# Loads of 112 rows in a convolution kernel with group norm: partitions 8 to 119, with a zero scale on the others

## The chip, the cores and the metric

The kernel runs on one core of a Trainium2 chip. The core has TensorE (PE), VectorE (DVE), ScalarE (ACT), GpSimd (POOL) and SyncE (SP), which here issues all DMAs; 16 DMA engines move data between the memory of the chip (HBM) and the on-chip memory of 128 partitions. The metric is the device time of one execution in microseconds. The kernel before takes 844.32 us, the median of 3 runs (842.21 to 863.63).

## What is computed

The input x has 32 images of 384 channels, 56 x 56 each, in float32. It is normalised in 32 groups of 12 channels, convolved channel by channel with a filter as tall as the image that wraps around, given a bias, and added to x.

```python
def _gn(v, G=32, eps=1e-5):
    g = v.reshape(B_, G, C_ // G, H_, W_)
    m = jnp.mean(g, axis=(2, 3, 4), keepdims=True)
    s = jnp.var(g, axis=(2, 3, 4), keepdims=True)
    return ((g - m) / jnp.sqrt(s + eps)).reshape(v.shape)

x_cat = jnp.concatenate([x, x[:, :, :-1, :]], axis=2)          # the wrap in H
out = conv_general_dilated(x_cat, weight, (1, 1), 'VALID', feature_group_count=C)
x + (out + bias[None, :, None, None])                          # conv of _gn(x)
```

## The kernel before

**Tiling.** The image rows (H = 56) lie on partitions. Two image sets lie side by side: one on partitions 8 to 63, the other on 64 to 119 (EDGE = 8, SIDE = 64, DATA = 112 rows). Partitions 0 to 7 and 120 to 127 hold no data; the host pads x with zeros there, so a load brings 128 rows. A unit is one group of 12 channels for 16 images (8 on each side); there are 64 units, two for a group. A unit is loaded and stored in two halves of 6 channels, 2688 floats to a partition each.

**The matmul.** The convolution in H is a product with a 128 x 128 matrix for each channel, two circulant blocks, one for each side. The matrices of a group lie in `runs` (two buffers). The taps come by DMA onto partitions 64 to 127 for output columns 64 to 119, and DVE's `lay_out` copies them to partitions 0 to 63 for the columns of the other side. The rows of this matrix on partitions 120 to 127 are not zero, nor are those on 0 to 7, so `xn`, the normalised input, has to be zero there.

**The stages of a unit**, each on its engine, in the order in which the engine's program is written:

- SP loads into one of six slots of `xt` (XS = 6). It waits until the store that emptied the slot has landed. One in-order queue holds stores, loads and the taps: for each half of unit u the store of (u, h) and then the load of (u + 5, h).
- DVE takes statistics (`bn_stats`, L280) three units ahead, 16 instructions a unit, and adds conv, bias and x for the even channels into `xt` (L304).
- POOL and PE combine the statistics over partitions with the matrices `neg_mean`, `avg` and `avg_dev`, whose columns for the outer partitions are zero, so that mean and variance are zero there. POOL's `newton` turns variance into `rstd` and `shift`: ACT takes the root of var + eps, DVE the reciprocal r0, and POOL does one Newton step with 1.5 from `three_halves`.
- ACT normalises `xt` into `xn` one unit ahead (L355), and moves the odd channels from PSUM to `kept` (L364), which POOL adds to `xt` (L248).
- PE multiplies the 12 channels into six banks of PSUM.

On the outer partitions DVE and POOL write bias and conv into the loaded tile too; the next 128-row load overwrites it with zeros. The store takes the 112 data rows alone.

**The start.** DVE sets eps (L272) and zeroes `runs`; POOL builds the three matrices and `three_halves` (L195 to L208) in a chain. ACT, PE and POOL wait for both through `consts_set`.

Of the kernel before, what the change touches and what calls it, by code (L numbers as in the profile page):

```python
# [13 lines left out]
GROUPS = 32  # L14
CG = C // GROUPS
EPS = 1e-5

# [3 lines left out]
P = 128  # L23
SIDE = P // PAR
EDGE = SIDE - H
DATA = PAR * H
# [11 lines left out]
BLOCK = SIDE * CG  # L38
RUN = H * CG
TAPS = PAR * BLOCK  # L40

XS = 6
# [12 lines left out]
def through(channels, u, c):  # L55

    return u * len(channels) + sum(k <= c for k in channels)

def build(nc, x, taps, bias, out):  # L60
    with ExitStack() as ctx:
        def sb(name, shape):
            return ctx.enter_context(nc.sbuf_tensor(name, shape, F32))
# [4 lines left out]
        def sem(name):  # L68
            return ctx.enter_context(nc.semaphore(name))

        xt = sb("xt", [P, XS, HALVES, FREE])
        xn = sb("xn", [P, NS, HALVES, FREE])
        kept = sb("kept", [P, KEEP, N])
        runs = sb("runs", [P, 2, TAPS])
# [4 lines left out]
        eps = sb("eps", [P, 1])  # L79
        warm = sb("warm", [P, 1])  # L80
        three_halves = sb("three_halves", [P, BP])
# [17 lines left out]
        x_loaded = [[sem(f"x_loaded{s}_{h}") for h in range(HALVES)] for s in range(XS)]  # L99
# [3 lines left out]
        consts_set = sem("consts_set")  # L103
# [38 lines left out]
        @block.sync  # L142
        def _(sp):
            def load(n, h):
                if n >= UNITS:
                    return
                if n >= XS:
                    sp.wait_ge(out_stored[n % XS][h], 16 * (n // XS))
                sp.dma_start(xt[:, n % XS, h, :], x[n, :, h, :]).then_inc(x_loaded[n % XS][h], 16)

            def load_taps(g):

                sp.dma_start(runs[SIDE:P, g % 2, BLOCK:BLOCK + RUN], taps[g]).then_inc(taps_loaded[g % 2], 16)

            def store(u, h):
                last = (h + 1) * CH - 1
                sp.wait_ge(dve_taken, through(DVE_CH, u, last))
                sp.wait_ge(pool_added, through(ACT_CH, u, last))
                sp.dma_start(out[u, :, h, :], xt[EDGE:EDGE + DATA, u % XS, h, :]).then_inc(out_stored[u % XS][h], 16)

            for h in range(HALVES):
                load(0, h)
            for h in range(HALVES):
                load(1, h)
            sp.wait_ge(runs_zeroed, 1)
            load_taps(0)
            sp.dma_start(bias_all[:], bias.broadcast_to([P, C])).then_inc(bias_loaded, 16)
            for n in range(2, XS):
                for h in range(HALVES):
                    load(n, h)  # L170
                if n == 3:
                    load_taps(1)

            for u in range(UNITS):
                for h in range(HALVES):
                    store(u, h)
                    g = u // PER_GROUP + 2
                    if h == 1 and u % PER_GROUP == PER_GROUP - 1 and g < GROUPS:
                        load_taps(g)

                    if u >= 1:
                        load(u - 1 + XS, h)
            for s in range(XS):
                for h in range(HALVES):
                    sp.wait_ge(out_stored[s][h], 16 * len(range(s, UNITS, XS)))

        @block.gpsimd
        def _(pool):
            link = itertools.count(1)

            def chained(ins):
                ins.then_inc(pool_link, 1)
                pool.wait_ge(pool_link, next(link))
# [4 lines left out]
            for m in (neg_mean, avg, avg_dev):  # L198
# [3 lines left out]
                for first in (EDGE, SIDE):  # L202
# [2 lines left out]
                                                    base=-first, pattern=[[0, H]], channel_multiplier=1))  # L205
                    chained(nc.gpsimd.affine_select(out=cols, in_=cols, compare_op=ALU.is_ge, fill=0.0,
                                                    base=first + H - 1, pattern=[[0, H]], channel_multiplier=-1))
            nc.gpsimd.memset(three_halves[:], 1.5).then_inc(consts_set, 1)  # L208
            pool.wait_ge(consts_set, 2)

            def add_means(n):
                r = n % RS
# [20 lines left out]
            def newton(n):  # L233
                r = n % RS
                pool.wait_ge(var_ready, n + 1)
                chained(nc.gpsimd.tensor_scalar(hv[:], var[:, r, :], EPS, -0.5, ALU.add, ALU.mult))  # L236
                pool.wait_ge(r0_ready, n + 1)
# [18 lines left out]
            for u in range(UNITS):  # L256
                n = u + LEAD_COEF
# [11 lines left out]

        @block.vector  # L270
        def _(dve):
            nc.vector.memset(eps[:], EPS).then_inc(consts_set, 1)  # L272
            nc.vector.memset(runs[:], 0.0).then_inc(runs_zeroed, 1)

            def stats(n, k0, k1):
# [8 lines left out]
            def lay_out(g):  # L284

                dve.wait_ge(taps_loaded[g % 2], 16 * (g // 2 + 1))
                side = runs[SIDE:P, g % 2, BLOCK:BLOCK + RUN]
                nc.vector.tensor_copy(runs[0:SIDE, g % 2, 0:RUN], side)  # L288
                nc.vector.tensor_copy(runs[0:SIDE, g % 2, RUN:BLOCK], side[:, 0:BLOCK - RUN]).then_inc(taps_laid, 1)  # L289

            def add_vars(n):
# [20 lines left out]
            invert(0)  # L312
            stats(1, ALL * 3 // 4, ALL)
            lay_out(0)
            stats(2, 0, ALL // 2)
            add_vars(1)
# [20 lines left out]
        def _(act):  # L337
# [26 lines left out]
                nc.scalar.activation(kept_of(u, c), bank_bw(c), ACT.Identity, bias=bias_of(u, c)  # L364
                                     ).then_inc(act_evicted, 1)

            act.wait_ge(consts_set, 2)
            nc.scalar.activation(warm[:], eps[:], ACT.Sqrt)
            negmean(0)
            root(0)  # L370
# [6 lines left out]
            for u in range(UNITS):  # L377
                n, m = u + LEAD_NORM, u + LEAD_COEF
# [22 lines left out]
        def _(pe):  # L401
# [26 lines left out]
                nc.tensor.matmul(bank(c), lay[:, :, c], channel_of(xn, u % NS, c), start=True, stop=True  # L428
                                 ).then_inc(conv_ready, 1)

            pe.wait_ge(consts_set, 2)
            for n in range(LEAD_COEF):
                mean(n)
                variance(n)
# [1 line left out]
            for u in range(UNITS):  # L436
                n = u + LEAD_COEF
# [39 lines left out]
```

## Time and profile before

| | |
|---|---|
| median of 3 runs | 844.32 us |
| the profiled execution | 843.1 us, of which its span 841.4 us |
| busy: PE, DVE, ACT, POOL | 706.6, 727.6, 661.6, 574.5 us |
| bytes moved | 336.57 MB, of which HBM read 181.86, written 154.14 |
| mean rate over the span | 400 GB/s |
| TensorE's granted clock, mean | 0.995 |

The busy time of an engine is its share of one profiled execution. The DMA share is the mean busy share of the 16 DMA engines; with that share near 1 the GB/s beside it is what they can do on that mix, and a rate divided by the share compares stretches in which the engines were not full. A waiting row names what was waited for, the total, the count and the longest. A row for a stretch lists its start and end, its length, then busy time and instructions of PE, PE's weight loads, DVE, ACT and POOL, and last the granted clock, the DMA share and GB/s.

### The profile page before, as it was taken

Reading aid. Unit: us, or ns where it says so; the run is one execution under the profiler, and the core shown is the slowest. Engines: PE = TensorE matmul, PEld = TensorE weight load, DVE = VectorE, ACT = ScalarE, POOL = GpSimd, SP = SyncE. Lnnn points to the kernel's source line nnn. Section 1 sums busy time; section 2 is a strip of 40 time slices with the busy share of each in tenths; the row PEclk is TensorE's granted clock in tenths of the full one; section 3 lists DMA queues with packets and bytes.
Section 4 is the critical chain, followed back from the end, with each engine's and each line's share of the span. In section 5 each row is a group of like instructions: output and inputs, shape, how many; then the busy total and the mean of one; then the engine's idle time right before and its main releaser. Section 6 shows DMA issues by size and latency. Waiting matters only on the chain.

```text
span 841.4 us, 8606 instructions
## 1 busy us (share of the span) xinstructions
PE 706.6 (84%) x1920; PEld 555.5 (66%) x1920; DVE 727.6 (86%) x1602; ACT 661.6 (79%) x1026; POOL 574.5 (68%) x1114
## 2 busy tenths in 40 slices
PE   0699889888887888988888988888988888987895
PEld 0477667666666666766666767666766667766684
DVE  7799988888888888889998899998888998898862
ACT  0799878777787777878878988887887887887893
POOL 3388667767676666766766776776776676775775
PEclk9999999999999999999999999999999999999998
DMA  8999999999999999999999999999999999999977
GB/s 349 411 350 400 411 411 414 416 422 409 412 413 396 402 402 390 398 403 410 414 418 415 417 413 419 425 418 420 418 414 419 422 418 414 410 420 404 391 243 248
DMA packets 37572, 336.57 MB, mean 400 GB/s; under 512 B 4624, under 2 KB 4752, under 8 KB 6800
## 3 DMA queue, kind: packets, MB, share of 16 engines
q1 hardware_dynamic: 37520, 336.02, 98.9%
q8 instruction: 15, 0.25, 0.1%
q14 instruction: 37, 0.30, 0.1%
HBM read 181.86 MB, written 154.14 MB: 399 GB/s over the span
## 4 chain that ended last, share of the span: by engine, by line
DMA 57%; DVE 19%; ACT 11%; issue 6%; POOL 5%; PE 1%; SPq 0%; POOLq 0%
DMA xt<-x 31%; DMA out<-xt 26%; DVE st L280 10%; ACT xn L355 7%; DVE xt L304 5%; ACT kept L364 3%; POOL xt L248 3%; DVE runs L289 2%; PE conv L428 1%; DVE runs L288 1%; POOL newt L240 0%; POOL newt L239 0%; POOL rstd L241 0%; POOL shift L242 0%; POOL newt L238 0%
## 5 line engine op out<-in xcount | busy, mean ns | idle before, releaser
L428 PE MATMUL conv<-xn,runs 128*128 128x448 f32 x1536 | 662.3, 574 | 64.7 <-ACT xn L355 48.7
L428 PEld LDWEIGHTS conv<-xn,runs 128*128 128x128 f32 x1536 | 511.3, 347 | 147.4 <-ACT xn L355 77.0
L280 DVE BATCH_NORM_STATS2 st<-xt 128x6 f32<-128x336 f32 x1024 | 451.9, 495 | 84.8 <-DMA xt<-x 83.3
L248 POOL TENSOR_TENSOR xt<-xt,kept 128x448 f32<-128x448 f32 x384 | 434.7, 1139 | 104.5 <-ACT kept L364 104.5
L355 ACT ACTIVATE xn<-xt,shift,rstd 128x672 f32<-128x672 f32 x512 | 462.7, 942 | 47.2 <-POOL shift L242 47.2
L304 DVE SCALAR_TENSOR_TENSOR xt<-conv,bias_all,xt 128x448 f32<-128x448 f32 x384 | 257.0, 669 | 17.9 <-PE conv L428 17.8
L364 ACT ACTIVATE kept<-conv,bias_all 128x448 f32<-128x448 f32 x384 | 232.8, 620 | 9.6 <-PE conv L428 9.4
L345 ACT ACTIVATE std<-var,eps 128x8 f32<-128x8 f32 x64 | 19.2, 301 | 97.3 <-DVE var L294 97.2
L404 PEld LDWEIGHTS p_mean<-msum,neg_mean 128*128 128x128 f32 x128 | 19.9, 193 | 94.5 <-POOL msum L217 80.2
L404 PE MATMUL p_mean<-msum,neg_mean 128*128 128x8 f32 x128 | 25.2, 269 | 59.2 <-POOL msum L217 59.2
L238 POOL TENSOR_TENSOR newt<-r 128x8 f32<-128x8 f32 x64 | 12.7, 198 | 62.1 <-DVE r L299 61.4
L236 POOL TENSOR_SCALAR hv<-var 128x8 f32<-128x8 f32 x64 | 12.6, 196 | 52.5 <-DVE var L294 49.9
L412 PEld LDWEIGHTS p_var<-st,avg 128*128 128x128 f32 x128 | 19.6, 192 | 35.4 <-POOL dev L231 35.0
L289 DVE COPY runs<-runs 64x96 f32<-64x96 f32 x32 | 29.2, 912 | 0.0
L288 DVE COPY runs<-runs 64x672 f32<-64x672 f32 x32 | 27.9, 872 | 1.2
L412 PE MATMUL p_var<-st,avg 128*128 128x32 f32 x128 | 26.6, 291 | 2.8 <-POOL dev L231 2.8
L227 POOL TENSOR_TENSOR dev<-st,nmean 128x16 f32<-128x16 f32 x128 | 25.6, 221 | 1.9 <-ACT nmean L340 1.9
L413 PE MATMUL p_var<-dev,avg_dev 128*128 128x32 f32 x128 | 25.3, 280 | 0.0
L214 POOL TENSOR_TENSOR mpart<-st 128x16 f32<-128x16 f32 x64 | 15.2, 237 | 7.6 <-DVE st L280 7.6
L340 ACT COPY nmean<-p_mean 128x8 f32<-128x8 f32 x64 | 9.5, 149 | 13.4 <-PE p_mean L404 13.2
L413 PEld LDWEIGHTS p_var<-dev,avg_dev 128*128 128x128 f32 x128 | 19.9, 196 | 0.0
L231 POOL TENSOR_TENSOR dev<-dev 128x32 f32<-128x32 f32 x64 | 15.2, 238 | 5.0
(31 smaller groups left out, 97.2 us busy)
## 6 DMA issues: line engine op xcount, KB each, us to landing
xt<-x SPq DMA_DIRECT2D x128, 1344.0 KB, 16.0
out<-xt SPq DMA_DIRECT2D x128, 1176.0 KB, 14.3
runs<-taps SPq DMA_DIRECT2D x32, 168.0 KB, 13.5
bias_all<-bias SPq DMA_DIRECT2D x1, 192.0 KB, 13.8
```

The lines of the kernel that those rows point to most:

```text
L227: ins = nc.gpsimd.tensor_tensor(d[:, h], means, nm, ALU.add)
L248: nc.gpsimd.tensor_tensor(cell, cell, kept_of(u, c), ALU.add).then_inc(pool_added, 1)
L280: ins = nc.vector.bn_stats(st[:, n % RS, h, b, :], xt[0:P, n % XS, h, b * ROW:(b + 1) * ROW])
L288: nc.vector.tensor_copy(runs[0:SIDE, g % 2, 0:RUN], side)
L289: nc.vector.tensor_copy(runs[0:SIDE, g % 2, RUN:BLOCK], side[:, 0:BLOCK - RUN]).then_inc(taps_laid, 1)
L304: nc.vector.scalar_tensor_tensor(out=cell, in0=bank_bw(c), scalar=bias_of(u, c), in1=cell, op0=ALU.add, op1=ALU.add).then_inc(dve_taken, 1)
L355: ins = nc.scalar.activation(xn[:, n % NS, :, part], xt[0:P, n % XS, :, part], ACT.Identity, scale=rstd[:, n % RS, b:b + 1], bias=shift[:, ...
L364: nc.scalar.activation(kept_of(u, c), bank_bw(c), ACT.Identity, bias=bias_of(u, c)).then_inc(act_evicted, 1)
L404: nc.tensor.matmul(p_mean[:, n % RS * BP:(n % RS + 1) * BP], neg_mean[:], msum[:, n % RS, :], start=True, stop=True).then_inc(mean_ready, 1)
L412: nc.tensor.matmul(dst, avg[:], squares, start=True, stop=False)
L413: nc.tensor.matmul(dst, avg_dev[:], dev[:, r, :], start=False, stop=True).then_inc(pvar_ready, 1)
L428: nc.tensor.matmul(bank(c), lay[:, :, c], channel_of(xn, u % NS, c), start=True, stop=True).then_inc(conv_ready, 1)
```

## The change

A load into a slot that has held data before covers rows 8 to 119 alone, on the same partitions as the stores. The first load into each slot still covers all 128 rows. The outer partitions are thus not cleared after that; bias and conv pile up on them. So that `xn` stays zero there, `eps` is 1e32 and `three_halves` is 0 on the outer partitions: r0 becomes 1e-16, the Newton step multiplies it by nearly nothing, and `rstd` is zero. `lay_out` leaves the columns of output partitions 0 to 7 as the zeros that `runs` was set to, so its first copy has 576 columns in place of 672.

```diff
@@ -146,7 +150,8 @@
                     return
                 if n >= XS:
                     sp.wait_ge(out_stored[n % XS][h], 16 * (n // XS))
-                sp.dma_start(xt[:, n % XS, h, :], x[n, :, h, :]).then_inc(x_loaded[n % XS][h], 16)
+                rows = slice(0, P) if n < XS else slice(EDGE, EDGE + DATA)
+                sp.dma_start(xt[rows, n % XS, h, :], x[n, rows, h, :]).then_inc(x_loaded[n % XS][h], 16)
 
             def load_taps(g):
 
@@ -205,8 +210,15 @@
                                                     base=-first, pattern=[[0, H]], channel_multiplier=1))
                     chained(nc.gpsimd.affine_select(out=cols, in_=cols, compare_op=ALU.is_ge, fill=0.0,
                                                     base=first + H - 1, pattern=[[0, H]], channel_multiplier=-1))
-            nc.gpsimd.memset(three_halves[:], 1.5).then_inc(consts_set, 1)
-            pool.wait_ge(consts_set, 2)
+            chained(nc.gpsimd.memset(eps[:], EPS))
+            chained(nc.gpsimd.memset(eps[P - 32:P], FAR))
+            chained(nc.gpsimd.memset(eps[P - 32:EDGE + DATA], EPS))
+            chained(nc.gpsimd.memset(eps[0:EDGE], FAR))
+            chained(nc.gpsimd.memset(three_halves[:], 1.5))
+            chained(nc.gpsimd.memset(three_halves[P - 32:P], 0.0))
+            chained(nc.gpsimd.memset(three_halves[P - 32:EDGE + DATA], 1.5))
+            nc.gpsimd.memset(three_halves[0:EDGE], 0.0).then_inc(consts_set, 1)
+            pool.wait_ge(consts_set, 1)
 
             def add_means(n):
                 r = n % RS
@@ -269,7 +281,6 @@
 
         @block.vector
         def _(dve):
-            nc.vector.memset(eps[:], EPS).then_inc(consts_set, 1)
             nc.vector.memset(runs[:], 0.0).then_inc(runs_zeroed, 1)
 
             def stats(n, k0, k1):
@@ -285,7 +296,7 @@
 
                 dve.wait_ge(taps_loaded[g % 2], 16 * (g // 2 + 1))
                 side = runs[SIDE:P, g % 2, BLOCK:BLOCK + RUN]
-                nc.vector.tensor_copy(runs[0:SIDE, g % 2, 0:RUN], side)
+                nc.vector.tensor_copy(runs[0:SIDE, g % 2, BLOCK - RUN:RUN], side[:, BLOCK - RUN:RUN])
                 nc.vector.tensor_copy(runs[0:SIDE, g % 2, RUN:BLOCK], side[:, 0:BLOCK - RUN]).then_inc(taps_laid, 1)
 
             def add_vars(n):
@@ -364,7 +375,7 @@
                 nc.scalar.activation(kept_of(u, c), bank_bw(c), ACT.Identity, bias=bias_of(u, c)
                                      ).then_inc(act_evicted, 1)
 
-            act.wait_ge(consts_set, 2)
+            act.wait_ge(consts_set, 1)
             nc.scalar.activation(warm[:], eps[:], ACT.Sqrt)
             negmean(0)
             root(0)
@@ -428,7 +439,7 @@
                 nc.tensor.matmul(bank(c), lay[:, :, c], channel_of(xn, u % NS, c), start=True, stop=True
                                  ).then_inc(conv_ready, 1)
 
-            pe.wait_ge(consts_set, 2)
+            pe.wait_ge(consts_set, 1)
             for n in range(LEAD_COEF):
                 mean(n)
                 variance(n)
```

(`FAR = 1e32` is new beside the other constants.)

On SP's queue, from the first store on (its source is `xt`, its target `out`; loads go from `x` to `xt`), the kernel before issues:

```order
L159 DMA out<-xt 112x2688 [waits pool_added,dve_taken] x3
L149 DMA xt<-x 128x2688 [waits out_stored0_0]
L159 DMA out<-xt 112x2688 [waits pool_added,dve_taken]
L153 DMA runs<-taps 64x672
L149 DMA xt<-x 128x2688 [waits out_stored0_1]
```

After the change the same place reads:

```order
L164 DMA out<-xt 112x2688 [waits pool_added,dve_taken] x3
L154 DMA xt<-x 112x2688 [waits out_stored0_0]
L164 DMA out<-xt 112x2688 [waits pool_added,dve_taken]
L158 DMA runs<-taps 64x672
L154 DMA xt<-x 112x2688 [waits out_stored0_1]
```

No DMA has moved and every wait is the same; each load that waits for a store has 112 rows where it had 128. The twelve loads ahead of this place are unchanged.

On POOL, at the end of the constants and before the first statistics are combined (`mpart`), the kernel before has:

```order
L206 AFFINE_SELECT avg_dev<-avg_dev 128x56 [waits pool_link]
L204 AFFINE_SELECT avg_dev<-avg_dev 128x56 [waits pool_link]
L206 AFFINE_SELECT avg_dev<-avg_dev 128x56 [waits pool_link]
L208 MEMSET three_halves 128x8 [waits pool_link]
L214 TENSOR_TENSOR mpart<-st 128x16 [waits stats_ready,consts_set]
```

And after the change:

```order
L211 AFFINE_SELECT avg_dev<-avg_dev 128x56 [waits pool_link]
L213 MEMSET eps 128x1 [waits pool_link]
L214 MEMSET eps 32x1 [waits pool_link]
L215 MEMSET eps 24x1 [waits pool_link]
L216 MEMSET eps 8x1 [waits pool_link]
L217 MEMSET three_halves 128x8 [waits pool_link]
L218 MEMSET three_halves 32x8 [waits pool_link]
L219 MEMSET three_halves 24x8 [waits pool_link]
L220 MEMSET three_halves 8x8 [waits pool_link]
L226 TENSOR_TENSOR mpart<-st 128x16 [waits stats_ready,consts_set]
```

Seven memsets are added to the chain at this one place; POOL's program behind it is unchanged.

## Rows read from the trace of the kernel before

**Rows 1.** The page: busy time by engine, packets and queue.

```profile
PE 706.6 (84%) x1920; PEld 555.5 (66%) x1920; DVE 727.6 (86%) x1602; ACT 661.6 (79%) x1026; POOL 574.5 (68%) x1114
...
DMA packets 37572, 336.57 MB, mean 400 GB/s; under 512 B 4624, under 2 KB 4752, under 8 KB 6800
...
q1 hardware_dynamic: 37520, 336.02, 98.9%
...
HBM read 181.86 MB, written 154.14 MB: 399 GB/s over the span
```

**Rows 2.** The page: the chain that ended last, shares by engine.

```profile
DMA 57%; DVE 19%; ACT 11%; issue 6%; POOL 5%; PE 1%; SPq 0%; POOLq 0%
```

**Rows 3.** DVE's waits (us, times, longest) and busy time, 100 to 780 us.

```profile
DVE st L280 <- DMA xt<-x: 76.3, 72, 2.4
...
100.00:780.00 680.00, 589.17 (x1596) 459.37 (x1596) 600.31 (x1330) 548.15 (x852) 473.40 (x909) 1.00 1.01 412
```

**Rows 4.** DMA to landing: loads from 40 us on, then the last five stores.

```profile
L149 SPq DMA_DIRECT2D xt<-x x116: 351/361/2477, 51.4 to 782.9; - x116
...
DMA to landing us min/median/max: 10.3/15.9/18.5
...
L159 SPq DMA_DIRECT2D out<-xt x5: 316/317/317, 817.2 to 835.3; - x5
...
DMA to landing us min/median/max: 5.3/5.3/5.5
```

**Rows 5.** The chain, one loop (start us, length us, what).

```profile
571.06 15.16 DMA out<-xt
586.24 15.94 DMA xt<-x
602.20 1.33 DVE st L280 x3
...
621.33 15.25 DMA out<-xt
```

**Rows 6.** The page: DMA issues, KB each; then all loads' landing, min/median/max.

```profile
xt<-x SPq DMA_DIRECT2D x128, 1344.0 KB, 16.0
out<-xt SPq DMA_DIRECT2D x128, 1176.0 KB, 14.3
runs<-taps SPq DMA_DIRECT2D x32, 168.0 KB, 13.5
...
DMA to landing us min/median/max: 5.8/16.0/32.4
```

**Rows 7.** Busy by stretch, clock, DMA share, GB/s: loads alone, refill, stores alone.

```profile
8.00:12.00 4.00, 0.00 (x0) 0.00 (x0) 4.00 (x11) 0.00 (x0) 0.00 (x0) 1.00 1.01 430
44.00:68.00 24.00, 22.31 (x66) 18.20 (x64) 23.91 (x55) 22.50 (x35) 19.85 (x38) 1.00 0.97 339
800.00:841.00 41.00, 31.55 (x85) 26.70 (x83) 19.04 (x33) 26.85 (x42) 27.18 (x38) 0.94 0.73 247
```

**Rows 8.** The same view: two mixed stretches.

```profile
200.00:400.00 200.00, 169.19 (x456) 131.29 (x456) 171.69 (x385) 156.54 (x244) 134.04 (x259) 1.00 1.01 404
400.00:600.00 200.00, 176.03 (x482) 138.66 (x482) 182.72 (x402) 164.89 (x257) 142.37 (x274) 1.00 1.01 418
```

**Rows 9.** DVE by line: busy us, mean ns.

```profile
L288 DVE COPY runs<-runs 64x672 f32<-64x672 f32 x32 | 27.9, 872 | 1.2
```

**Rows 10.** The first 15 us in order of time (start us, length us).

```profile
1.58 0.10 POOL L200 MEMSET neg_mean<- 128x8 f32 x1
1.75 0.10 POOL L201 MEMSET neg_mean<- 128x8 f32 x1
...
6.17 0.10 POOL L208 MEMSET three_halves<- 128x8 f32 x1
6.30 0.20 ACT L368 ACTIVATE warm<-eps 128x1 f32<-128x1 f32 x1 [4.23 <-POOL three_halves L208]
...
13.42 0.23 POOL L214 TENSOR_TENSOR mpart<-st 128x16 f32<-128x16 f32 x1 [7.15 <-DVE st L280]
...
14.68 0.17 ACT L340 COPY nmean<-p_mean 128x8 f32<-128x8 f32 x1 [8.18 <-PE p_mean L404]
```

More of the change, by code:

```diff
@@ L16 @@
 EPS = 1e-5
+FAR = 1e32
 PAR = 2
```

## The prediction

> **What bounds the kernel now.** I read the page first. The DMA queue that carries all loads and stores keeps the 16 engines busy for 98.9% of the span, while the busiest compute engine, DVE, works 86% of it [rows 1]. The chain that ended last agrees: 57% of it is DMA and only 19% is DVE [rows 2]. So this is a kernel whose transfers set the pace, unless the DMA share is queueing behind something else. Three further views say that it is not.
>
> The waits of DVE between 100 and 780 us have a single entry, the x load, with 76.3 us; DVE is busy 600.3 of those 680 us, so all but 680 - 600.3 - 76.3 = 3.4 us of its idle time is that wait [rows 3]. The DMA share of that stretch is 1.01 (full) at 412 GB/s [rows 3]. And a DMA takes 15.9 us from issue to landing for a load in the middle of the kernel, 15.2 and 16.0 us in a piece of the chain, but only 5.3 us for a store when nothing else is under way at the end [rows 4, 5]. Ten of those 16 us are thus time in the queue. The chain repeats one loop every four units: store issued at 571.06, landed, its slot's load landed at 602.20, then DVE, POOL, ACT and POOL again until the next store at 621.33 [rows 5]. That is 50.3 us, of which 31.1 is DMA and 19.1 compute. Without a queue the loop would be about 19 + 5.3 + 5.8 = 30 us (5.8 is the shortest landing of a load [rows 6]), or 7.6 us a unit. So neither the number of slots nor latency is the limit: the bytes are.
>
> One unit carries two loads of 1344 KB, two stores of 1176 KB and half a taps load of 168 KB [rows 6], 5124 KB = 5.247 MB. At 412 GB/s that is 12.73 us. DVE needs 600.3 us of work in the same 680, and 680 / 12.73 = 53.4 units, so 11.24 us a unit. These two numbers, 12.73 and 11.24, are the case: the DMA can lose up to 1.5 us a unit before DVE sets the pace.
>
> **The change part by part.** *The loads.* Twelve loads (six slots, two halves) keep 128 rows. The other 128 - 12 = 116 lose 16 rows of 128, which is 168 KB or 0.172 MB each: 116 x 0.172 = 19.96 MB of the 336.57 MB [rows 1, 6]. The order on SP's queue and its waits stay as they were. If the rate stays 412 GB/s, the saving is 19.96 MB / 412 GB/s = 48.4 us. The unit falls to 5.247 - 0.344 = 4.903 MB, 11.90 us. DVE's 11.24 still fits under it, with 0.66 us to spare where 1.5 us was.
>
> *The rate.* This is where it could fail. Loads of 128 rows, before any store is issued (8 to 12 us), run at 430 GB/s with share 1.01, so 426 per full share. Stores alone, which are 112 rows from partition 8 (from 800 us on), run at 247 GB/s with share 0.73: 338 per full share, a fifth less [rows 7]. Part of the 0.73 is that they come singly, but the rate per busy share should not fall for that. So something about a 112-row transfer costs time when it runs by itself, and the trace can't say whether it is the direction (a store) or the shape. The loads now get that shape. There is one hint against fear: in the steady stretches, where stores are nearly half the bytes, the whole mix makes 418 GB/s at 1.01 (414 per full share) from 400 to 600 us, and 404 from 200 to 400 [rows 8]. If loads take their 426 there, the stores must take 2.408 MB / (5.247 / 414 - 2.839 / 426) = 2.408 / 6.009 us = 401 GB/s, not 338. The penalty of the shape is mostly gone once the queue is deep. In contrast, from 44 to 68 us, when stores begin and the queue is refilled, the mix makes only 339 at 0.97 [rows 7].
>
> The cost of the shape is therefore bounded from both sides. Nothing: 48.4 us are saved. All of it, as in the tail: a load of 1.204 MB at 338 takes 3.56 us against 1.376 / 426 = 3.23, so each of the 116 is 0.33 us longer and the kernel 38 us slower. At the stores' steady 401 GB/s it is 3.00 us, and the saving is 116 x 0.23 = 27 us; but that charges to stores everything that slows the mix, some of which (the refill, memory, loads themselves) falls on loads already. I take the value nearest to the steady rows, a loss of 5 us out of the 48.4. It is the deep queue that decides, and the change leaves it deep: 11.90 against DVE's 11.24.
>
> The Trainium skill, "SBUF — State Buffer", section "Door 1: The DMA port swizzle", speaks against this change. It says that partitions share 16 ports of eight partitions each, that a transfer is as fast as the ports it reaches, and its table puts partitions 0 to 7 and 120 to 127 on four ports that each serve four other partitions in 8 to 119; by its arithmetic twelve ports still carry eight rows and nothing is saved. The tail's 338 GB/s agrees with it in direction; the steady 414 doesn't show it, because loads and stores alternate there and no port is asked for all the time. By that rule alone the sum would be about the time of before (R2 below).
>
> *The taps copy.* Each of the 32 layouts copies 576 columns in place of 672: 872 ns x 96 / 672 = 0.12 us, 4 us of DVE in all, 0.06 us a unit [rows 9]. DVE waits for DMA, so this is nothing on the path; it widens DVE's spare time to 0.7 us.
>
> *The constants.* POOL sets eps and three_halves with eight chained memsets where one stood, and DVE loses one. A small memset on POOL takes 0.10 us and starts 0.17 us after the one before it, so consts_set comes 7 x 0.17 = 1.2 us later, at about 7.5 us. Behind it wait POOL's first mpart, which waits for statistics until 13.42 anyway, and ACT's warm-up at 6.30, whose next work is at 14.68 [rows 10]. Hidden with 6 us of cover; 1.2 us if that were gone. The zero in rstd on the outer partitions adds no instruction.
>
> *DVE's waits that return.* With 0.7 us of spare a unit instead of 1.5, a burst in which DMA is quick no longer helps: DVE can't catch up. From 200 to 400 us DMA ran at 404 and from 400 to 600 at 418 [rows 8], so the spare varies by 5.247 x (1/404 - 1/418) = 0.43 us a unit, less than 0.7. I allow 2 us.
>
> The sum against the profiled span: 841.4 - 48.4 + 5 + 2 = 800.0 us of span. The profiled execution itself took 1.7 us more than its span (843.1), and the median of the runs is 844.3, so 1.7 to 2.9 us are added: about 802. I say 801.
>
> **The rivals.** *R1, DVE becomes the bound.* If the loads came for nothing, the span would be at least 841.4 - 76.3 - 4 = 761 us. That is below 800, so DVE alone can't stop the gain. But the two paces are only 6% apart, and when DVE holds the stores back the queue drains, transfers run singly and their rate falls towards that of 44 to 68 us. For: that stretch exists, with DVE busy 23.9 of 24 us [rows 7]. Against: it ended by itself at 68 us. Half of the gain would be gone: 841.4 - 24 = 817, a time of 819. The DMA share would be 0.95 to 0.98 and DVE's wait for x small.
>
> *R2, the shape is paid for in full by the ports.* A 112-row load takes as long as a 128-row one did (373 GB/s in place of 426). The bytes fall and the time doesn't: 841 to 844 us. For: the tail's 338. Against: the mixed stretches. The rate on the page would fall from 400 to 316.6 MB / 841 us = 376 GB/s at a full share.
>
> *R3, slower.* Loads of 112 rows collide with each other as stores do when they are alone, at more than 3.23 us each; that is the point from which it decides. At the tail's 338 GB/s the price is 38 us: 879 to 882. For it speaks that now no transfer in the queue has the regular 128-row shape. Against it: the queue is mostly full and half of it is the other direction, as it is for stores now.
>
> **How the numbers follow.** A measurement of this kernel can tell about 2% from no change, so faster is below 827.4 and slower above 861.2. Forecast (bytes decide, 790 to 810): 0.60. R1 (810 to 827): 0.18. R2 (827 to 861): 0.12. R3 (over 861): 0.10. The first two are faster: 0.78. The low end of the range: a steady rate of 425 GB/s, the loads' 426, in place of 412 would take off a further 20 us, but with DVE at 11.2 of then 11.5 us a unit some 4 of it would come back; 784. The high end takes in R1 and the first part of R2, up to the saving being a third: 832. That leaves out some 0.19.
>
> **What would show it.** The page should list 316.6 MB, reads about 162 MB, DMA share in the steady stretch still 1.00 or more, and 405 to 418 GB/s there. DVE's wait for x should fall from 76 to about 35 to 45 us in the steady part, and the loop of the chain from 50.3 to 47 us. A load's landing should shorten from 15.9 to about 14.5 us. The startup should be the same to 1 us. R1 shows a share below 1 and DVE near 95%; R2 and R3 show a full share at under 385 GB/s with DVE's wait for x as long as now or longer. The prediction is wrong if the mean time of a byte in the queue changes with the shape of the load.

## The result and the profile after

The changed kernel takes 889.4 us (median, 886.8 to 905.6), the kernel before beside it 848.5 us. The ratio is 1.050, with a 95% interval of 1.038 to 1.062: slower by 5%, where a gain of 5% was forecast. Executions of one kernel scatter (842 to 864 us before), so ratios here compare the faster executions of each. The profiled execution's span is 889.2 us.

The page after, lines that answer to [rows 1, 2, 6]; the second is GB/s in 40 slices of the span:

```profile
PE 726.2 (82%) x1920; PEld 562.1 (63%) x1920; DVE 716.6 (81%) x1601; ACT 663.0 (75%) x1026; POOL 575.8 (65%) x1121
...
GB/s 353 412 315 356 353 365 382 371 360 367 341 367 385 381 361 377 403 391 339 347 351 333 324 343 345 352 354 366 346 356 341 340 379 364 360 371 392 396 253 252
DMA packets 35716, 316.61 MB, mean 356 GB/s; under 512 B 4624, under 2 KB 4752, under 8 KB 6800
...
q1 hardware_dynamic: 35664, 316.07, 98.8%
...
DMA 71%; DVE 10%; POOL 7%; ACT 6%; issue 3%; PE 1%; SPq 0%; POOLq 0%
...
xt<-x SPq DMA_DIRECT2D x116, 1176.0 KB, 17.5
```

The bytes are as forecast, 316.61 MB. The 16 engines are as full as before, 98.8%, but they move 356 GB/s where they moved 400. The rate wanders between 324 and 403 after the start. DMA's share of the chain has gone from 57 to 71%. A load takes 17.5 us to land, not the 14.5 that were forecast.

DVE's wait from 100 to 780 us, then stretches of the same execution (columns as in [rows 3, 7]):

```profile
DVE st L291 <- DMA xt<-x: 126.7, 92, 3.3
...
8.00:12.00 4.00, 0.00 (x0) 0.00 (x0) 4.00 (x11) 0.00 (x0) 0.00 (x0) 1.00 1.01 427
100.00:780.00 680.00, 565.93 (x1481) 432.69 (x1482) 550.51 (x1239) 511.25 (x793) 440.07 (x844) 0.95 1.01 359
400.00:600.00 200.00, 164.09 (x421) 123.71 (x420) 153.98 (x350) 144.13 (x224) 123.58 (x238) 0.93 1.01 343
850.00:889.00 39.00, 29.31 (x78) 24.95 (x78) 16.75 (x28) 24.92 (x38) 25.82 (x36) 0.96 0.71 239
```

Against [rows 3]: DVE's wait for x is 126.7 us, not 76.3, and the steady rate 359, not 412. The first row, full loads alone, is nearly unchanged (427, 430 before), and so is the tail of stores alone (239 at a share of 0.71, which is 337 per full share; 338 before). The loss lies in the stretch where 112-row loads and stores share the queue: 4.903 MB at 359 GB/s is 13.7 us a unit, against 12.7 before.

The kept traces also have one record for each packet, and nearly all packets are rows of 10,752 bytes. From 100 to 780 us such a packet takes 404 ns at the median in both kernels. But 27% of them take over 500 ns after the change, where 5% did before, and their mean is 481 ns, not 419. That ratio, 1.148, is the ratio of the two rates (412 / 359). So the engines do not stand idle between packets; some packets of the same size take longer.

### The profile page after: what moved, and what is told of

The parts are those of the page before. It is cut to its first block, busy times and chain, and to the rows that moved or that the text cites. A ratio compares the mean times of both kernels' runs of the same rounds, so it can differ in the third digit from the quotient of the medians.

```text
span 889.2 us, 8612 instructions
## 1 busy us (share of the span) xinstructions
PE 726.2 (82%) x1920; PEld 562.1 (63%) x1920; DVE 716.6 (81%) x1601; ACT 663.0 (75%) x1026; POOL 575.8 (65%) x1121
## 2 busy tenths in 40 slices
DMA packets 35716, 316.61 MB, mean 356 GB/s; under 512 B 4624, under 2 KB 4752, under 8 KB 6800
## 3 DMA queue, kind: packets, MB, share of 16 engines
q1 hardware_dynamic: 35664, 316.07, 98.8%
## 4 chain that ended last, share of the span: by engine, by line
DMA 71%; DVE 10%; POOL 7%; ACT 6%; issue 3%; PE 1%; SPq 0%; POOLq 0%
DMA xt<-x 40%; DMA out<-xt 32%; DVE st L291 6%; ACT xn L366 4%; POOL xt L260 4%; DVE xt L315 3%; ACT kept L375 2%; PE conv L439 1%; DVE runs L299 0%; POOL newt L252 0%; POOL newt L251 0%; POOL rstd L253 0%; POOL newt L250 0%; POOL shift L254 0%; DVE runs L284 0%
## 5 line engine op out<-in xcount | busy, mean ns | idle before, releaser
L439 PE MATMUL conv<-xn,runs 128*128 128x448 f32 x1536 | 688.1, 592 | 104.0 <-ACT xn L366 92.7
L315 DVE SCALAR_TENSOR_TENSOR xt<-conv,bias_all,xt 128x448 f32<-128x448 f32 x384 | 256.5, 668 | 18.9 <-PE conv L439 18.8
L415 PEld LDWEIGHTS p_mean<-msum,neg_mean 128*128 128x128 f32 x128 | 23.5, 216 | 86.6 <-POOL msum L229 67.2
L415 PE MATMUL p_mean<-msum,neg_mean 128*128 128x8 f32 x128 | 25.2, 270 | 48.4 <-POOL msum L229 48.4
L250 POOL TENSOR_TENSOR newt<-r 128x8 f32<-128x8 f32 x64 | 12.7, 199 | 75.9 <-DVE r L310 75.4
L299 DVE COPY runs<-runs 64x576 f32<-64x576 f32 x32 | 29.8, 932 | 2.0 <-DMA runs<-taps 1.1
L252 POOL TENSOR_TENSOR newt<-newt,three_halves 128x8 f32<-128x8 f32 x64 | 13.0, 204 | 5.0
(37 smaller groups left out, 98.8 us busy)
## 6 DMA issues: line engine op xcount, KB each, us to landing
out<-xt SPq DMA_DIRECT2D x128, 1176.0 KB, 15.7
xt<-x SPq DMA_DIRECT2D x116, 1176.0 KB, 17.5
```

Of the source, the lines that this page charges most:

```text
L299: nc.vector.tensor_copy(runs[0:SIDE, g % 2, BLOCK - RUN:RUN], side[:, BLOCK - RUN:RUN])
L315: nc.vector.scalar_tensor_tensor(out=cell, in0=bank_bw(c), scalar=bias_of(u, c), in1=cell, op0=ALU.add, op1=ALU.add).then_inc(dve_taken, 1)
L415: nc.tensor.matmul(p_mean[:, n % RS * BP:(n % RS + 1) * BP], neg_mean[:], msum[:, n % RS, :], start=True, stop=True).then_inc(mean_ready, 1)
```

## The experiments

**Which edit.** The first run undoes the loads alone.

```diff
-rows = slice(0, P) if n < XS else slice(EDGE, EDGE + DATA)
+rows = slice(0, P)
```

> The changed kernel with every load at 128 rows again; eps, three_halves, the constants in POOL and the shorter taps copy stay as changed. If the loads alone are the cause (S, D or Q): the time of the kernel before, 840 to 848 us, steady rate about 412 GB/s. If the startup or the other edits cost something: over 855.

848.6 us, ratio 1.005 (0.999 to 1.011). The other edits cost nothing that can be measured; all of the loss comes from the loads. (The profiled execution took 873.9 us, so the steady rate of 412 that was expected can't be read from it.)

**What a DMA of each shape can do.** This kernel has no compute. It reads and writes the same arrays by the same queue, in most phases with five DMAs under way. Each kernel of DMAs alone in this document was executed once. The phases:

```python
PHASES = [  # kind, load rows, at, store rows, at, under way, count
    ("L", P, 0, None, 0, 5, 16), ("L", DATA, EDGE, None, 0, 5, 16),
    ("S", None, 0, P, 0, 5, 16), ("S", None, 0, DATA, EDGE, 5, 16),
    ("M", P, 0, DATA, EDGE, 5, 32), ("M", DATA, EDGE, DATA, EDGE, 5, 32), ...
```

> DMA alone, no compute; the output is not the reference's. After 12 loads of 128 rows come 12 phases, each drained before the next: loads of 128 rows; loads of 112 rows (partitions 8 to 119); stores of 128; stores of 112; then alternating stores and loads: 128-row loads with 112-row stores (as before), 112 with 112 (as after), 128 with 128, 112-row loads with 128-row stores; loads of 64 rows from the same source onto partitions 0 to 63, then onto 32 to 95; and the 112/112 mix again with 3 and with 8 DMAs under way instead of 5. Theory S (the shape costs: transfers of 112 rows collide in the on-chip memory, whichever their direction): per full share, 128-row loads and stores 420 to 426 GB/s, 112-row loads and stores both 340 to 380, the mixes with one regular side 400 to 420, 128/128 420 to 426, 112/112 340 to 375; 64 rows at 32 about twice as fast as at 0. Theory D (stores are slow as such): stores 340 at either height, 112-row loads 426, 112/112 no slower per byte than 128/112. Theory Q (depth of the queue decides): the 112/112 mix is slow at 3 and reaches 400 or more at 8.

One row inside each phase, in the order of the text above; the 128/128 mix (417) is left out (columns: stretch, length, POOL, clock, DMA share, GB/s):

```profile
46.00:94.00 48.00, 0.00 (x0) 1.00 1.01 427
100.00:162.00 62.00, 0.00 (x0) 1.00 1.01 292
169.00:216.00 47.00, 0.00 (x0) 1.00 1.01 422
223.00:278.00 55.00, 0.00 (x0) 1.00 0.97 330
290.00:380.00 90.00, 0.00 (x0) 1.00 1.01 419
395.00:495.00 100.00, 0.00 (x0) 1.00 1.00 362
615.00:720.00 105.00, 0.00 (x0) 1.00 1.01 370
730.00:778.00 48.00, 0.00 (x0) 1.00 1.02 207
785.00:808.00 23.00, 0.00 (x0) 1.00 1.01 428
815.00:915.00 100.00, 0.00 (x0) 1.00 1.01 368
925.00:1022.00 97.00, 0.00 (x0) 1.00 1.01 375
```

Loads: 427 GB/s at 128 rows, 292 at 112. Stores: 422 and 330. So the shape costs and the direction doesn't: Theory D falls with the third row. A 112-row load is hit even harder than a store, 292 against 330, where 340 to 380 was expected for both. The mix of before makes 419, that of after 362, and its mirror image (112-row loads, 128-row stores) 370 with the same bytes as before. The last two are averages over a rise that I did not see at first: in slices of about 20 us the mix of after goes from 341 to 376 and the mirror image from 343 to 390.

The two rows of 207 and 428 are the cleanest pair: the same 64 source rows to partitions 0 to 63 make 207, to 32 to 95 they make 428. Only the place in the on-chip memory differs. In the packet records a row takes 839 ns at the median in the first of the two and 404 in the second; in the 112-row loads it takes 574, in the 128-row loads 405.

The Trainium skill, "SBUF — State Buffer", section "Door 1: The DMA port swizzle", gives the table behind that pair: 0 to 63 reach eight of 16 ports, 32 to 95 all of them. The trace agrees, 207 against 428.

Depth does not remove the loss: 368 with three under way, 375 with eight, though both rise too (344 to 383, and 343 to 410).

**Stores at 128 rows in the kernel.** From the kernel before, with an output array of 128 rows:

```diff
-sp.dma_start(out[u, :, h, :], xt[EDGE:EDGE + DATA, u % XS, h, :])
+sp.dma_start(out[u, :, h, :], xt[:, u % XS, h, :])
```

> The kernel before with stores of 128 rows too (the output array has 128 rows, the host drops 16). Bytes 358.6 MB, 6.5% more. Theory S: the rate in the steady part rises from 412 to 422 to 426, the tail (stores alone) from 338 to about 420 per full share; a unit takes 5.59 MB / 424 = 13.2 us in place of 12.73, the kernel about 868 us. Theory D: tail still 338 per share, steady rate at most 412, 890 us or more.

```profile
100.00:780.00 680.00, 572.31 (x1530) 441.37 (x1530) 576.88 (x1275) 525.93 (x818) 454.70 (x868) 0.99 1.01 421
832.00:872.00 40.00, 30.29 (x81) 25.34 (x79) 18.69 (x33) 26.23 (x40) 26.48 (x38) 0.96 0.70 291
```

873.5 us, ratio 1.030 (1.024 to 1.035), for 6.5% more bytes. The steady rate is 421, and the tail of stores alone makes 291 at a share of 0.70, 416 per full share, against 338 in [rows 7]. The tail that I had read as possibly the direction was the shape.

**Half the loads, and the mirror image.** Only the first half of each unit at 112 rows:

```diff
-rows = slice(0, P) if n < XS else slice(EDGE, EDGE + DATA)
+rows = slice(0, P) if n < XS or h == 1 else slice(EDGE, EDGE + DATA)
```

> The changed kernel, but only the loads of the first half of a unit have 112 rows, those of the second 128. Bytes 326.6 MB. If every 112-row load costs its own extra time (as measured, 45 us for 116 of them, against 48 us that fewer bytes should have saved): half of it, ratio about 1.025, 866 us. If the collisions need loads and stores that all have the irregular shape, and one regular DMA in four sets them straight: nothing lost and 24 us saved, about 820.

Ratio 1.073 (1.057 to 1.089), 919.8 us: worse than all of them at 112. The page says why: 357 GB/s on average, the rate of the changed kernel (356), with 10 MB more to move. So the price is not one per 112-row load. I read it as a state of the whole queue that half the loads are enough to bring about; what brings it about is not shown. Both expectations missed: the 866 us from a price for each load, and the 820 us from the idea that one regular DMA in four would set the rest straight.

The mirror image has the stores of 128 rows above on top of the changed kernel.

> The changed kernel with stores of 128 rows: one direction regular, the other not, the mirror image of the kernel before, and within 1% its bytes (loads 2 x 1176 KB and stores 2 x 1344 KB a unit). Theory that one irregular direction is harmless: ratio 1.00 to 1.02. By the DMA-only phases (370 GB/s for this mix against 419 for the mix of before): 5.247 MB / 370 = 14.2 us a unit in place of 12.7, so about 930 us, ratio 1.10.

Four executions took 891, 896, 926 and 936 us, the kernel before beside them 839 to 868. The profiled one (891) runs at 358 GB/s from 100 to 330 us and at 404 from 350 to 840. Two of the four are near the 930 us expected from the DMA-only 370, two are not. One irregular direction is thus not harmless when it is the loads; and the state can change within one execution.

**Where the rows lie.** More phases, six shapes of loads first:

```python
PHASES = [  # pattern of (kind, rows, at, source row), under way, count
    ([("L", 112, 8, 8)], 5, 16), ([("L", 112, 8, 0)], 5, 16), ([("L", 112, 0, 8)], 5, 16),
    ([("L", 96, 16, 8)], 5, 16), ([("L", 64, 8, 8)], 5, 16), ([("L", 48, 32, 8)], 5, 16), ...
```

> DMA alone again, 12 phases after the 12 full loads; its output is not the reference's. Six kinds of loads alone, 16 each: 112 rows to partitions 8 to 119; the same but from source rows 0 to 111; the same to partitions 0 to 111; 96 rows to 16 to 111; 64 rows to 8 to 71; 48 rows to 32 to 79. Then 12 times a load of 64 rows to 32 to 95 with one of 24 rows to 8 and one of 24 to 96. Then mixes: 112-row stores with 128-row loads; with 112-row loads; store, 112-row load, store, 128-row load; 112-row stores with 64-row loads to 32; and with 64-row loads to 8. For the pattern with 112- and 128-row loads in turn, a model with whole packets waiting for each other gives 353, below the 362 of all 112 and the 419 of all 128. Rival H (the source side): source rows 0 to 111 at 420. Rival E (only the rows that start at 8 are bad): 112 rows to 0 and 96 to 16 at 420.

```profile
46.00:110.00 64.00, 0.00 (x0) 1.00 1.01 280
118.00:175.00 57.00, 0.00 (x0) 1.00 1.01 304
184.00:245.00 61.00, 0.00 (x0) 1.00 1.01 290
254.00:310.00 56.00, 0.00 (x0) 1.00 1.01 258
320.00:368.00 48.00, 0.00 (x0) 1.00 1.01 203
575.00:672.00 97.00, 0.00 (x0) 1.00 1.00 379
682.00:780.00 98.00, 0.00 (x0) 1.00 1.01 388
790.00:860.00 70.00, 0.00 (x0) 1.00 1.00 383
876.00:960.00 84.00, 0.00 (x0) 1.00 0.99 345
```

The first five rows are loads alone, the sixth and seventh the mixes with 112-row loads and with both kinds, the last two those with 64-row loads to 32 and to 8. (The 48-row phase ran at 251, the three-piece loads at 254, the mix with 128-row loads at 420.) No start and no source helps 112 or 96 rows: 280, 304, 290, 258. Rivals H and E fall. What no phase separates is the side on which 112 rows collide: each still goes between HBM and the on-chip memory, and H changed only the first source row. That it is the on-chip side, as with 64 rows, is argued.

The port-bound 64 rows at 8 make 203, as forecast. The mix that alternates 112- and 128-row loads makes 388 here, between the two pure mixes (379 and 420). In the kernel with half of the loads at 112 rows the same order made only 357, and that difference is open. My model of whole packets that wait for each other had put it below both, at 353; it misses. The 112/112 mix, 362 before, averages 379 here and has come to 416 in its last 22 us.

**The same in the kernel**, with 64-row loads (48 data rows of each repeated load are left out):

```diff
-rows = slice(0, P) if n < XS else slice(EDGE, EDGE + DATA)
+rows = slice(0, P) if n < XS else slice(8, 72)      # and slice(32, 96)
```

> The changed kernel, but repeated loads bring only 64 rows to partitions 32 to 95, so 48 data rows are left out of each load; all engines work as before. 3.87 MB a unit. Port theory: loads are regular, DMA at about 400 needs 9.7 us a unit, DVE's 11.3 sets the pace: 765 to 790 us.

> The same number of rows and bytes, but to partitions 8 to 71. Port theory: a 64-row load takes 0.688 MB / 207 = 3.3 us in place of 1.6, as long as a 128-row load, so about 12.7 us a unit or more: 840 to 900 us. If only bytes and rows count: the same as with partitions 32 to 95.

747.6 us to 32 and 748.1 to 8: no difference, and both expectations (765 to 790, and 840 to 900) missed. I had used the rate of such loads alone for a kernel in which they alternate with stores; the DMA-only mixes had made 383 and 345. The rows from 100 to 650 us, to 32 and to 8:

```profile
100.00:650.00 550.00, 522.91 (x1495) 434.52 (x1494) 547.35 (x1244) 513.15 (x798) 447.78 (x844) 1.00 0.99 351
100.00:650.00 550.00, 522.21 (x1492) 433.90 (x1491) 546.82 (x1243) 512.61 (x796) 448.70 (x844) 1.00 1.01 351
```

DVE works 547 of 550 us in both. (The chain that ended last runs through ACT for 52% and hardly through DVE; that DVE is the bound is read from its busy time.) The time of this pair could not tell the places apart, but the landing does: a load takes 9.3 us to 32 and 12.0 us to 8. The pair measured two other things. With DVE as the bound the span is 745 us. And to 32 the DMA share is 0.99 at 351 GB/s, where the same mix alone makes 383: a share near 1 says that something is always under way, and not that the engines can do no more. So the GB/s beside such a share is not always what they can do on that mix, as I wrote ahead of the prediction.

**Can the bad state end?** The next kernel keeps 112/112 up for 96 DMAs and tries groups and two queues.

> DMA alone, the output is not the reference's; stores always 112 rows. After the 12 full loads: 112-row loads from SP's queue beside stores from ACT's queue (16 each, 3 and 2 under way); 128-row loads beside such stores in the same way; then on SP's queue alone: store and load in turn at 112/112, 96 of them (to see whether the rate holds or wanders); two stores then two loads at 112/112; four and four with 8 under way; store and load in turn with 128-row loads. Theory S: 112/112 in turn 350 to 370 as before, wandering between 330 and 400; groups of one direction are worse, 300 to 340, since more engines are then at the same side's ports at once, and four and four worst; two queues make no difference of more than 5% (the same 16 engines). Rival Q: two queues bring 112/112 to 400 or more, and then it is the order on one queue that costs.

The first two rows are the two-queue phases, then 112/112 early and late, then groups of two and of four:

```profile
50.00:110.00 60.00, 0.00 (x0) 1.00 1.01 409
150.00:235.00 85.00, 0.00 (x0) 1.00 1.01 419
256.00:304.00 48.00, 0.00 (x0) 1.00 1.01 350
352.00:520.00 168.00, 0.00 (x0) 1.00 1.01 429
540.00:645.00 105.00, 0.00 (x0) 1.00 1.01 333
660.00:770.00 110.00, 0.00 (x0) 1.00 1.00 316
```

After about 90 us the 112/112 mix stands at 429 GB/s, for 168 us. In the packet records of that stretch 99% of the rows take 404 to 407 ns; from 256 to 304 us 35% took over 500. So the shape doesn't have to cost anything, and Theory S, which expected 350 to 370 throughout, was wrong on that. My explanation is that at a steady beat the 16 engines shift against each other until no two want the same part of the memory at once. It is argued: the records show that packets stop taking longer, but not which engine serves which row. Groups of one direction are worse over their 105 and 110 us, 333 and 316, as Theory S says. And two queues make 409 at once, 419 with 128-row loads. For 112/112 that is 17% over the 350 of one queue, where Theory S allowed 5%: Rival Q's sign is there. With 128-row loads one queue does as well, 417 to 420 in the phases above.

Why doesn't the kernel reach that state? Two things differ: it has taps loads (64 rows of 2688 bytes) in the queue, and compute, which may let the beat falter.

> DMA alone on SP's queue, the output is not the reference's. After the 12 full loads three phases: 112-row stores and 112-row loads in turn, 96 of them, 5 under way, with a taps load (64 rows of 2688 bytes to partitions 64 to 127) after every eighth as in the kernels; the same without taps loads and 4 under way; 48 of 112-row stores with 128-row loads, with taps loads. The long 112/112 phase of the run before began at about 350 GB/s and stood at 429 from its 90th us on: the engines had shifted against each other until none met another at a port. Theory T (the taps loads break this up in the kernel): the first phase never settles, 340 to 380 to its end; the second settles at 425 to 430 after about 100 us; the third holds 410. Theory K (only the kernel's compute, which lets the queue run low, breaks it up): the first phase settles at 420 or more as well, and the second too. Theory F (four under way are too few): the second does not settle.

112/112 with taps loads at the end of its phase; without them, early and late; 128/112 with taps:

```profile
195.00:370.00 175.00, 0.00 (x0) 1.00 1.01 352
400.00:500.00 100.00, 0.00 (x0) 1.00 1.01 350
550.00:645.00 95.00, 0.00 (x0) 1.00 1.01 421
700.00:820.00 120.00, 0.00 (x0) 1.00 1.01 419
```

With taps the mix stays near 352 for all 337 us. Without them it settles at 421, about 160 us after the phase began; it had four under way and not five, but five settled too in the kernel above. The mix of before takes the taps without harm, 419. So far Theory T. In the kernel, the taps loads after the second group are left out (and DVE's wait for them with it):

```diff
-if h == 1 and u % PER_GROUP == PER_GROUP - 1 and g < GROUPS:
+if h == 1 and u % PER_GROUP == PER_GROUP - 1 and g < 2:
```

> The changed kernel without the 30 taps loads after the first two (every group is computed with the taps of group 0 or 1, all copies and matmuls stay; 5.2 MB less). Theory T: the steady rate rises from 360 to 420 or more once settled, DVE's pace of 11.3 us a unit is nearly reached, 770 to 800 us. Theory K: the rate stays at 340 to 390 and the time at 870 to 895 (5.2 MB at 360 GB/s is 14 us).

Ratio 1.023 (1.008 to 1.037), 867.2 us. Of the 22 us, 14 are the missing bytes. The steady rate is 367, with slices from 320 to 406. Theory T's 770 to 800 us fails, and the time is just under Theory K's 870 to 895. But K's claim that only compute matters had failed in the phases. So the taps are one disturbance, and in the kernel something else is enough of one without them. That it is compute's faltering demand was not isolated.

**Two queues in the kernel.** Stores are issued by ACT, loads and taps by SP:

```diff
+def store(u, h):      # in ACT's program
+    act.wait_ge(dve_taken, through(DVE_CH, u, last))
+    act.wait_ge(pool_added, through(ACT_CH, u, last))
+    act.dma_start(out[u, :, h, :], xt[EDGE:EDGE + DATA, u % XS, h, :]).then_inc(...)
 ...
     normalize(n, 2, 4)
+    store(u - 1, 1)
 ...
     normalize(n, 7, BP)
+    store(u, 0)
```

This does more than add a queue: loads no longer stand behind a store that waits for DVE and POOL, the taps stand behind both loads of a unit, and a store goes out at a place in ACT's program.

> DMA alone, the output is not the reference's: 24 loads on SP's queue (3 under way) beside 24 stores of 112 rows on ACT's queue (2 under way), four times: 112-row loads, 128-row loads, 112-row loads with a taps load after every fourth, 128-row loads with the same. In the two-queue phases before, 112/112 made 406 to 412 GB/s at once, where one queue made 350 for its first 60 us. Theory Q2 (on two queues each engine changes between a store's and a load's packets, so that fewer engines are at one side's ports at once): 400 to 412 in the third phase as well, and 415 to 422 with 128-row loads. Theory T: taps loads bring the third phase down to 340 to 370.

112/112 without taps, 112/112 with taps, 128/112 with taps:

```profile
110.00:170.00 60.00, 0.00 (x0) 1.00 1.01 429
355.00:430.00 75.00, 0.00 (x0) 1.00 1.01 381
520.00:590.00 70.00, 0.00 (x0) 1.00 1.01 418
```

Again the taps loads hold the 112/112 mix down (429 to 381, and 368 in the 70 us after), and hardly the other. That is less than the 400 to 412 of Theory Q2 and more than the 340 to 370 of Theory T.

> The changed kernel with the stores issued from ACT's queue (the store of a unit's second half a few instructions into the next unit), loads and taps on SP's. Q2: 4.903 MB / 405 = 12.1 us a unit, 800 to 825 us, ratio 0.95 to 0.98. If compute's stalls or the taps undo it as on one queue: 870 to 900. If ACT, which now waits for POOL before it issues, becomes the bound: 850 to 900 with a DMA share below 0.97.

> The kernel before with the stores issued from ACT's queue. Q2: 5.247 MB / 420 = 12.5 us a unit in place of 12.73, 825 to 840 us, ratio 0.98 to 0.995, slower than the same with 112-row loads.

With 112-row loads: 861.8 us, ratio 1.023 (1.004 to 1.042), where 800 to 825 was expected. With 128-row loads: 833.1 us, ratio 0.989 (0.983 to 0.994), 1% less than the kernel before and as expected. From 100 to 780 us, the first with 112-row loads, the second with 128, and DVE's waits in the latter:

```profile
100.00:780.00 680.00, 577.33 (x1561) 451.38 (x1560) 558.89 (x1302) 536.14 (x833) 463.29 (x884) 0.98 1.01 377
```

```profile
100.00:780.00 680.00, 593.10 (x1620) 468.55 (x1620) 592.94 (x1352) 556.69 (x864) 481.85 (x918) 0.99 1.01 418
...
DVE runs L282 <- DMA runs<-taps: 89.4, 28, 5.6
...
DVE st L274 <- DMA xt<-x: 6.4, 7, 2.4
```

Two queues lift the steady rate from 359 to 377 and from 412 to 418. The gain comes with the split, whatever the loads, and the 112-row loads still lose. Which part of the split brings it was not separated: with 128-row loads the DMA-only phases show no gain from a second queue, so the freed order of the loads is a rival. DVE now waits for the taps (89.4 us, and 118.1 with 112-row loads), which stand behind loads on SP's queue; with the DMA share at 1.01 I take that wait to be in the place of the one for x, but no run moved the taps to test it.

## Why the prediction was wrong

**What bounds the kernel: right.** The bytes' way through the 16 engines did set the time, and still does. The share near 1 did not prove it, as the 64-row loads show; DVE's wait for x, 76.3 and then 126.7 us, and the packet times do.

**The bytes: right.** 19.96 MB fewer, 316.61 on the page.

**The rate: wrong, and this is the step that failed.** I wrote that the penalty of the shape is mostly gone once the queue is deep, and took 5 us for it. The steady rate fell from 412 to 359 instead. A unit of 4.903 MB then takes 13.66 us, not 11.90, and over the 58 units with shorter loads that is 102 us in place of the 5. Less the 48.4 us of fewer bytes, it makes the kernel 54 us slower; the spans differ by 889.2 - 841.4 = 47.8.

The reason that I gave fails with it: with three, five and eight DMAs under way the new mix makes 368, 362 and 375, so a deep queue does not take the penalty away. The row I leaned on, 414 per full share in the mix, was true, but it was the property of a mix in which loads are regular. The load's own row, 426, told nothing of a load at 112 rows. The only row with that shape alone was the tail (338), and it was right about stores: 330 at a share of 0.97. The refill (339 at 0.97) was no such row, since its loads have 128 rows; DVE works 23.9 of its 24 us, as with the 64-row loads, where the same low rate stands beside a share near 1.

That the DMA-only 362 comes so near the kernel's 359 is partly luck: the same mix averaged 379 in another run and stands at 429 once settled, and the kernel stays near the rate at which such a stream starts.

R3 took the tail's rate and named the collisions of 112-row loads, with a 38 us price; I gave it 0.10. I had argued against it that half of the queue is the other direction; DMA alone shows that it isn't enough. Its number came near (879 to 882), but its sum was only half right: it charged the loads alone, at 338, and the unchanged stores now take longer as well (15.7 us to landing, 14.3 before).

**R1: not met.** A kernel that DVE bounds takes 745 us, not 761, and DVE was further from being the bound, not nearer: 550.5 of 680 us.

**R2, the ports: half right.** The Trainium skill's rule on ports is borne out by 207 and 428 for 64 rows. For 112 rows it would give no less than 373 GB/s by my estimate, the rate at which such a load takes as long as one of 128 rows at 426. 292 alone is worse than that, and 429 in the settled mix better. So neither counting ports nor my rows of the mix of before gives the time; the same mix makes 350 or 429 with nothing changed but the time since it began. My reason for the steady 414, that no port is asked for all the time, is shown by no run.

**The small terms.** The constants were as written:

```profile
L299 DVE COPY runs<-runs 64x576 f32<-64x576 f32 x32 | 29.8, 932 | 2.0 <-DMA runs<-taps 1.1
L300 DVE COPY runs<-runs 64x96 f32<-64x96 f32 x32 | 14.2, 444 | 0.0
...
14.64 0.17 ACT L351 COPY nmean<-p_mean 128x8 f32<-128x8 f32 x1 [7.05 <-PE p_mean L415]
```

ACT's warm-up ran 1.1 us later (7.39) and the first nmean at 14.64, where it had been at 14.68 [rows 10]. The taps copy did not get shorter by 0.12 us: it takes 932 ns, not 872 [rows 9]. The second one, which reads and writes the same 96 columns as before, fell from 912 to 444 ns. Why, no run shows. Both are off the path.

## What to carry to other kernels

A transfer's rate belongs to its shape, to the shapes beside it in the queue, and here also to how long the stream has run undisturbed. Before taking rows off a transfer, find a stretch of the trace in which the new shape is alone. If it is slow, take that as a warning and not as a price: 112-row loads make 292 alone and 362 between stores. A kernel of DMAs alone, with the new mix, costs one run; read it in slices of time, since its average can hide a rise. Padding that makes all 128 partitions take part can be cheaper than the bytes it adds: 116 of 128 loads with an eighth fewer bytes cost 5% of the time here.

## What was not expected of the hardware

- Loads of 112 rows alone run at 280 to 304 GB/s, stores of 112 rows at 330, and at 427 and 422 with 128 rows.
- An alternating 112/112 stream starts at about 350 GB/s and after 90 to 160 us stands at 421 to 429 (two executions). With a small taps load after every eighth DMA it stayed near 352 for over 300 us (one execution).
- Stores on ACT's queue and loads on SP's move more than the same DMAs on one queue (409 against 350 at the start of a 112/112 stream), though the 16 engines are the same. The settled stream on one queue makes more than either, 429, and with 128-row loads there is no such difference.
- TensorE's mean granted clock was 0.964 after and 0.995 before: with DVE's longer waits for x, PE is busy 164.1 of the 200 us from 400 to 600, where it was 176.0, and the granted clock there is 0.93, where it was 1.00 [rows 8], so part of that stretch is at the lower of its two levels, 1.2 GHz. A conv matmul takes 592 ns, not 574. It isn't on the path: DVE's wait for conv is 18.8 us, 17.8 before.
